# One-hot look-ups of a DLRM tower: whole-table one-hots, ids for two tables at once, two look-up banks, embedding copies on two engines

## The reference

```python
e = jnp.stack([tbl_0[ids[:, 0]], ..., tbl_25[ids[:, 25]]], axis=1)      # 2048 x 26 x 128
combined = jnp.concatenate([dense[:, None, :], e], axis=1)              # 2048 x 27 x 128
interactions = jnp.einsum('bnd,bmd->bnm', combined, combined)
z = jnp.concatenate([dense, interactions[:, _TRIU_I, _TRIU_J]], axis=1)
h = jnp.concatenate([z, dense], axis=1)
h = jnp.maximum(h @ W_top1 + b_top1, 0.0)
h = jnp.maximum(h @ W_top2 + b_top2, 0.0)
y = h @ W_top3
```

## Time and profile before

| | us |
|---|---|
| median of 3 runs | 602.59 (599.72 to 607.67) |
| the profiled execution | 605.72 |
| its span | 603.9 |
| mean granted clock of TensorE | 0.822 of full speed |

### The profile page before, as it was taken

The page is one execution under the profiler, slowest core; times in us unless marked ns, Lnnn a source line. Parts: engine busy times, 40 slices in busy tenths (PEclk is TensorE's granted clock), DMA queues, the critical chain, the costliest instruction groups (busy, mean ns, idle before and its releaser), DMA issues.

```text
span 603.9 us, 13994 instructions
## 1 busy us (share of the span) xinstructions
PE 433.2 (72%) x6369; PEld 389.7 (65%) x6369; DVE 263.3 (44%) x258; ACT 207.4 (34%) x313; POOL 253.8 (42%) x261
## 2 busy tenths in 40 slices
PE   3773277766788677787778778786777867787927
PEld 3672157655767667676667767675676766777827
DVE  5981035671544424535244434554154442465221
ACT  3550023443313333234222433233332333335713
POOL 7787545374423445154351644345433344500000
PEclk9886557987868788888787888896887878889978
DMA  8923113031102111031110311121111211101010
GB/s 202 243 55 104 39 32 99 21 108 37 27 25 83 45 33 41 18 92 33 27 45 16 101 34 27 37 86 47 29 26 29 85 42 33 41 7 58 4 58 1
DMA packets 21909, 32.79 MB, mean 54 GB/s; under 512 B 8030, under 2 KB 14846, under 8 KB 21850
## 3 DMA queue, kind: packets, MB, share of 16 engines
q0 software_dynamic: 8288, 16.83, 11.0%
q1 hardware_dynamic: 13562, 15.06, 8.8%
HBM read 28.24 MB, written 3.68 MB: 53 GB/s over the span
## 4 chain that ended last, share of the span: by engine, by line
PE 56%; issue 16%; DVE 12%; ACT 9%; another core or an unknown queue 6%; DMA 1%; SPq 0%; DVEq 0%
PE hot_ps L617 23%; PE gram_ps L642 11%; DVE one_hot L503 9%; PE mlp_ps L649 6%; PE transpose_ps L593 5%; PE mlp_ps L650 5%; PE mlp_ps L651 5%; ACT embed_t L424 4%; ACT embed_t L379 3%; PE hot_ids_ps L599 2%; DVE packed_lo L507 1%; DVE units L489 1%; DMA bounce<-units 1%; DMA rows<-bounce 1%
## 5 line engine op out<-in xcount | busy, mean ns | idle before, releaser
L351 POOL DMA_INDIRECT rows<-table,ids_sb x256 | 252.9, 988 | 272.9 <-PE transpose_ps L593 199.4
L617 PE MATMUL hot_ps<-one_hot,table_hi 125*128 125x256 f32 x640 | 200.2, 338 | 65.7 <-ACT embed_t L424 43.6
L503 DVE TENSOR_TENSOR one_hot<-hot_ids_ps,row_numbers_sb 125x1024 fp32r<-125x1024 f32 x160 | 192.4, 1236 | 110.9 <-PE hot_ids_ps L599 59.4
L617 PEld LDWEIGHTS hot_ps<-one_hot,table_hi 125*128 125x128 f32 x640 | 142.2, 222 | 81.3 <-DVE one_hot L503 46.0
L617 PE MATMUL hot_ps<-one_hot,table_lo 125*128 125x256 f32 x640 | 185.4, 315 | 0.0
L617 PEld LDWEIGHTS hot_ps<-one_hot,table_lo 125*128 125x128 f32 x640 | 143.5, 224 | 0.0
L642 PE MATMUL gram_ps<-embed_t 128*27 128x27 f32 x4096 | 77.3, 205 | 67.0 <-issue 66.1
L642 PEld LDWEIGHTS gram_ps<-embed_t 128*27 128x27 f32 x4096 | 58.8, 117 | 88.2 <-issue 85.3
L379 ACT COPY embed_t<-transpose_ps 128x512 f32<-128x512 f32 (+1 forms) x80 | 85.3, 1066 | 79.9 <-PE transpose_ps L593 51.1
L424 ACT COPY embed_t<-hot_ps 128x256 f32<-128x256 f32 x80 | 54.8, 684 | 148.2 <-PE hot_ps L617 82.1
L489 DVE COPY_PREDICATED units<-late_sb,gram_ps 128x208 f32<-128x208 int32 x32 | 35.1, 1098 | 121.2 <-ACT units L418 115.3
(11 more groups left out here) (49 smaller groups left out, 314.6 us busy)
## 6 DMA issues: line engine op xcount, KB each, us to landing
rows<-table,ids_sb POOLq DMA_INDIRECT x256
embed_t<-table SPq DMA_DIRECT2D x8, 448.0 KB
bounce<-units SPq DMA_DIRECT2D x8, 448.0 KB
scratch<-bounce SPq DMA_DIRECT2D x7, 378.0 KB
rows<-dense SPq DMA_DIRECT2D x16, 64.0 KB
scratch<-table SPq DMA_DIRECT2D x2, 448.0 KB
scratch<-w SPq DMA_DIRECT2D x1, 512.0 KB
scratch<-w_units SPq DMA_DIRECT2D x2, 252.0 KB
```

The source lines that it names most:

```text
L351: nc.gpsimd.indirect_dma_start(rows[:, t2, f, :], None, tables[table], bass.IndirectOffsetOnAxis(ids_sb[:, slot, table:table + 1], 0)).the ...
L503: nc.vector.tensor_tensor(one_hot[:, n % RING], ids_over, numbers_over, ALU.is_equal).then_inc(one_hot_ready, 1)
L617: last = nc.tensor.matmul(hot_ps[:, 0:GROUP], table[:, k % HOT, step, :], one_hot[:, (2 * k + half) % RING, j, :], start=(step == 0 and ta ...
```

## The change

- A one-hot is made for a whole table in one instruction of 2048 elements; the ring holds two whole tables. An H step is a whole table, and the order of the steps is written anew.
- The ids come in rows of 512, two tables side by side. One selector matmul spreads a pair; it stands ahead of the pair-before's second table.
- Even tables are looked up in `hot_ps`, odd ones in the half of `mlp_ps` that the odd MLP stages use. A table waits for the copy of the table two before, and odd tables and odd MLP stages wait for each other.
- Q0, Q2 and Q4 are copied out by ACT, Q1 and Q3 by DVE, with a semaphore each.
- To make room, `w1d_sb` goes (its piece is loaded into `scratch`, after `w2` is split), and one half of `hidden2` lies in `scratch`.

```diff
-RING = 3
-AHEAD = 2
+RING = 2
+PAIR = 2
+PAIRS = HOT // PAIR
+PAIR_ROWS = PAIRS * GROUPS
...
 STEPS = [
-    "D0 S0 M0 G0 Q0 G1 M1 G2 Q1 W0 M2 G3 H0 M3 H1 Q2 H2 W1 H3 Q3 H4 H5 W2 Q4 H6 H7".split(),
-    "G0 H8 G1 H9 Q0 H10 G2 H11 M4 G3 H12 Q1 H13 W3 M5 H14 Q2 H15 W4 M6 H16 Q3 H17 W5 Q4 H18 H19".split(),
+    "D0 S0 M0 G0 Q0 G1 M1 G2 Q1 W0 M2 W1 G3 H0 M3 Q2 W2 H1 Q3 H2 W3 Q4 H3".split(),
+    "G0 H4 W4 G1 Q0 H5 W5 M4 G2 Q1 M5 H6 G3 M6 Q2 H7 Q3 H8 Q4 H9".split(),
 ]
...
-FIRST_STEPS = "H0 H1 H2 Q0 H3 H4 H5 H6 Q1 H7 H8 H9 H10 Q2 H11 H12 H13 H14 Q3 H15 H16 H17 Q4 H18 H19".split()
+FIRST_STEPS = "H0 Q0 H1 H2 Q1 H3 H4 Q2 H5 H6 Q3 H7 H8 Q4 H9".split()
...
-    one_hot = sb("one_hot", [HOT_P, RING, HALF_STEPS, GROUP], F32R)
+    one_hot = sb("one_hot", [HOT_P, RING, HOT_STEPS, GROUP], F32R)
...
+        def hot_bank(k):
+
+            return hot_ps[:, 0:GROUP] if k % 2 == 0 else mlp_ps[:, 1, 0:GROUP]
...
                     sp.dma_start(scratch[:, :, :], w2.rearrange("(c p) h -> p c h", p=P)).then_inc(weights_loaded, 16)
+
+                    sp.wait_ge(weights_lo, CHUNKS + 1)
+                    sp.dma_start(w1d_sb, w1_dense).then_inc(weights_loaded, 16)
                     sp.dma_start(w1a_sb, w1_again).then_inc(weights_loaded, 16)
...
-                    sp.wait_ge(weights_lo, CHUNKS + 1)
-                    sp.wait_ge(w1_summed, 1)
+                    sp.wait_ge(weights_lo, len(pieces))
...
-            def make_one_hot(n):
...
+            def make_one_hot(k):
+
+                if k >= RING:
+
+                    dve.wait_ge(hot_ready, k - RING + 1)
+                if k % PAIR == 0:
+                    dve.wait_ge(hot_ids_ready, k // PAIR + 1)
+                ids = hot_ids_ps[0:HOT_P, None, k % PAIR * GROUP:(k % PAIR + 1) * GROUP]
+                nc.vector.tensor_tensor(one_hot[:, k % RING], ids.to_broadcast([HOT_P, HOT_STEPS, GROUP]),
+                                        row_numbers_sb[:, :, None].to_broadcast([HOT_P, HOT_STEPS, GROUP]),
+                                        ALU.is_equal).then_inc(one_hot_ready, 1)
+
+            def embed_copy(g, buf, t2, u):
+
+                dve.wait_ge(transposed, TRANSPOSE_USES * g + t2 * TILE_BANKS + u + 1)
+                nc.vector.tensor_copy(embed_target(g, t2, u), embed_source(t2, u)).then_inc(odd_copied, 1)
...
-                        elif step == "H" and LOOKUPS * (g + 1) + n + AHEAD < GROUPS * LOOKUPS:
-                            make_one_hot(LOOKUPS * (g + 1) + n + AHEAD)
+                        elif step == "Q" and n % 2 == 1:
+                            embed_copy(*next_tile(g, buf, t2), n)
+                        elif step == "H" and HOT * (g + 1) + n + RING < GROUPS * HOT:
+                            make_one_hot(HOT * (g + 1) + n + RING)
...
-            def broadcast_ids(k):
-
-                row = k % HOT * GROUPS + k // HOT
-                nc.tensor.matmul(hot_ids_ps[0:HOT_P, 0:GROUP],
-                                 selector[:, row:row + 1].to_broadcast([HOT * GROUPS, HOT_P]), hot_ids_sb[:, :],
+            def broadcast_ids(pair):
+
+                row = pair % PAIRS * GROUPS + pair // PAIRS
+                nc.tensor.matmul(hot_ids_ps[0:HOT_P, :],
+                                 selector[:, row:row + 1].to_broadcast([PAIR_ROWS, HOT_P]), hot_ids_sb[:, :],
                                  start=True, stop=True).then_inc(hot_ids_ready, 1)
...
+                k = g * HOT + n
+
+                pe.wait_ge(one_hot_ready, k + 1)
...
+                if k % PAIR == PAIR - 1 and k + 1 < GROUPS * HOT:
+
+                    broadcast_ids(k // PAIR + 1)
+                if k >= 2:
+
+                    pe.wait_ge(hot_copied, k - 1)
+                if k % 2 == 1 and odd_bank["stages"]:
+
+                    pe.wait_ge(mlp_copied, odd_bank["stages"])
+                for step in range(HOT_STEPS):
                     for table in (table_hi, table_lo):
...
                 pe.wait_ge(mlp_copied, MLP_USES * g + need + 1)
+                if m % 2 == 1:
+
+                    pe.wait_ge(hot_copied, odd_bank["tables"])
+                    odd_bank["stages"] = MLP_USES * g + m + 2
```

More of the change, by code:

```diff
@@ L199, in dlrm_tower @@
         transposed = sem("transposed")
-        embed_copied = sem("embed_copied")
+        even_copied = sem("even_copied")
+        odd_copied = sem("odd_copied")
         gram_ready = sem("gram_ready")
@@ L420, in hot_copy @@
             def hot_copy(g, k, buf):
-                act.wait_ge(hot_ready, LOOKUPS * g + 2 * (k + 1))
+                act.wait_ge(hot_ready, HOT * g + k + 1)
                 out = over_group(g, HOT_FEATURE + k)
-                nc.scalar.copy(out, hot_ps[:, 0:GROUP].rearrange("p (t b) -> p t b", t=TILES)).then_inc(hot_copied, 1)
+                nc.scalar.copy(out, hot_bank(HOT * g + k).rearrange("p (t b) -> p t b", t=TILES)).then_inc(hot_copied, 1)
             def group(g, buf, steps, mlp_before=True):
@@ L430, in group @@
                             late_columns(g, buf, t2 * TILE_ROUNDS + n // PARTS)
-                        elif step == "Q":
+                        elif step == "Q" and n % 2 == 0:
                             embed_copy(*next_tile(g, buf, t2), n)
-                        elif step == "H" and n % 2 == 1:
-                            hot_copy(g + 1, n // 2, 1 - buf)
+                        elif step == "H":
+                            hot_copy(g + 1, n, 1 - buf)
                         elif step == "D" and mlp_before:
@@ L462, in _ @@
             for step, n in [(x[0], int(x[1:])) for x in FIRST_STEPS]:
-                if step == "H" and n % 2 == 0 and n // 2 + 1 < HOT:
-                    split_hi(n // 2 + 1)
-                elif step == "H" and n % 2 == 1:
-                    hot_copy(0, n // 2, 0)
-                elif step == "Q":
+                if step == "H":
+                    if n + 1 < HOT:
+                        split_hi(n + 1)
+                    hot_copy(0, n, 0)
+                elif n % 2 == 0:
                     embed_copy(0, 0, 0, n)
@@ L563, in _ @@
             for step, n in [(x[0], int(x[1:])) for x in FIRST_STEPS]:
-                if step == "H" and n % 2 == 0 and n // 2 + 1 < HOT:
-                    split_lo(n // 2 + 1)
                 if step == "H":
-                    make_one_hot(n + AHEAD)
+                    if n + 1 < HOT:
+                        split_lo(n + 1)
+                    make_one_hot(n + RING)
+                elif n % 2 == 1:
+                    embed_copy(0, 0, 0, n)
             dve.wait_ge(late_loaded, 16)
@@ L581, in _ @@
         def _(pe):
+            odd_bank = {"tables": 0, "stages": 0}
             def transposes(g, buf, t2, u, first=False):
@@ L588, in transposes @@
                 pe.wait_ge(gathered[t2][u], 16 * len(gathers(u)) * (g + 1))
-                if not (first and use < 2):
-                    pe.wait_ge(embed_copied, TRANSPOSE_USES * g + use - 1)
+                if u >= 2 or not first:
+                    done, at = (TILES * g + t2, u - 2) if u >= 2 else (TILES * g + t2 - 1, u - 2 + TILE_BANKS)
+                    if at % 2 == 0:
+                        pe.wait_ge(even_copied, even_copies(done, at + 1))
+                    else:
+                        pe.wait_ge(odd_copied, odd_copies(done, at + 1))
                 for i, f in enumerate(features(u)):
@@ L621, in look_up @@
                 last.then_inc(hot_ready, 1)
-                if half == 0 and k + 1 < GROUPS * HOT:
-                    pe.wait_ge(one_hot_ready, 2 * (k + 1))
-                    broadcast_ids(k + 1)
+                if k % 2 == 1:
+                    odd_bank["tables"] = k + 1
             def gram(g, buf, t2, n, first):
@@ L682, in mlp @@
                         for c in range(H2_CHUNKS):
-                            last = nc.tensor.matmul(out[:, t:t + 1], hidden2[:, c, t * P:(t + 1) * P], w3_sb[:, c:c + 1],
+                            last = nc.tensor.matmul(out[:, t:t + 1], hidden2[c][:, t * P:(t + 1) * P], w3_sb[:, c:c + 1],
                                                     start=(c == 0), stop=(c == H2_CHUNKS - 1))
@@ L763 @@
     given = {
-        "dense": a["r_dense_features"], "ids": a["ids"], "hot_ids": np.ascontiguousarray(a["ids"].T[HOT_TABLES]).reshape(HOT * GROUPS, GROUP),
+        "dense": a["r_dense_features"], "ids": a["ids"], "hot_ids": np.ascontiguousarray(a["ids"].T[HOT_TABLES].reshape(PAIRS, PAIR, GROUPS, GROUP).transpose(0, 2, 1, 3)).reshape(
+            PAIR_ROWS, PAIR * GROUP),
         "row_numbers": np.arange(HOT_ROWS, dtype=np.float32).reshape(HOT_P, HOT_STEPS),
```

68 lines of the change are left out of this document (28 added, 40 removed).

## The result

The changed kernel takes **609.13 us** (median of 20 runs, 604.14 to 620.14) where the kernel before takes 601.93 (20 runs). The ratio is 1.0113, 95% interval 1.0083 to 1.0142: a loss of 1.1% that the measurement can tell from none. I had forecast a small gain, 600 against 602.6.

A forecast was written before the change was run, and what follows sets the result against it. PE bounds the kernel, over a quarter of its time waiting, with each group's second tile hanging on gathers. Six steady groups by -0.5 is -3, plus 1, minus 2: 4 us less, 601.7, scaled 598.6, rounded up to 600; range 568 to 624.

The forecast's parts named there:

- Ends: Step on the run's start and last group: plus 1 us for weights, 0 for first tables and grams, minus 2 at the end.
- 1 us of a range of 0 to 3.15: Start: the first weights piece loads later, once `w2` is split, delaying DVE's later one-hots; 1 us taken.
- two copies (2.4 us) come on top: First ten tables, DVE-paced: two added copies, 2.4 us, counted 0 because the first grams stand among the first 48 gathers anyway.
- 2 us less for the edge without one-hots: Last group: no one-hots are left to make at the edge, so 2 us less.
- 10 us of cover: Group edge: SyncE's pack, twice some 3.15 us from the predicated copy on, has 10 us of cover.
- The edge wait of 4 to 8 us: Each group's edge: PE waits 4 to 8 us for DVE, where 2.2 stood before.
- The two late one-hots at the edge: Group's end: two one-hots see PE's signals late out of the gather run, by 1.7 to 6 us; 3.7 taken.
- The DVE copy at 1.2 us: Embedding copies moved to DVE: a 128x512 copy out of PSUM takes near 1.2 us, ACT's time for the same access.
- The steady group at no gain to speak of: Steady groups, tile 1 at 35.0 against 35.4 us and tile 0 at 0: a gain of 0.4 to 0.5 us each.
- The hold is PE's own waiting (faster): Rival, gather runs: signals are late because PE stands at a semaphore, two banks end it; 572 us, chance 0.35.
- The queue of DVE at the edge (slower): Rival, group edge: `dense_lo` stands behind four one-hots, two late; 620 us, chance 0.25; sign: DVE's "remote" waits before the last two.
- Two banks give nothing: Rival, look-ups: 2.3 us of short waits are only renamed to one-hot waits; 603 us, chance 0.40 together with the forecast's case.

The follow-up runs named there:

- c1: The changed kernel itself, unaltered, in the free condition (kernel before 430.48 us there): 443.42 us, ratio 1.0323.
- c2: The kernel before, unaltered, traced in the same free condition: 432.36 us (one run).
- e7: Changed kernel with the last weight pieces' steps (w2 and two more) moved later, behind grams; held condition: 614.93 us, ratio 1.0170 to the kernel before.
- e10: Kernel before with two look-up banks alone, no other part of the change; held condition: 626.28 us, ratio 1.0345.
- e5: Changed kernel with tile 1's last gram ahead of M5 and H6 on every engine; free condition: 436.34 us, ratio 1.0170 to the kernel before.
- e8: e6 and e7 together, with the first tables' two odd embedding copies on ACT; held condition: 589.95 us, ratio 0.9731 to the kernel before.
- e6: Changed kernel with e5 and e1 together and DVE's packed split ahead of both last one-hots; free condition: 408.69 us, ratio 0.9508 to the kernel before.
- e3: Changed kernel with a single look-up bank, each table waiting for ACT's copy of the one before; free condition: 447.63 us, ratio 1.0458.
- e13: e10's kernel with GpSimd's gathers left out, SyncE loading consecutive rows instead; free condition: 429.78 us, ratio 0.9991 to the kernel before.
- e11: Kernel before with GpSimd's 256 gathers left out, SyncE loading consecutive rows instead; free condition: 435.03 us, ratio 1.0105.
- e1: Changed kernel with the dense split moved behind M6 and the packed split ahead of the last look-up; free condition: 439.87 us, ratio 1.0258.

## Why the prediction was wrong

The sum by its own terms, between the same marks, in us:

| stretch | forecast | held | free (c1 less c2) |
|---|---|---|---|
| start, to group 2 | +0.5 (1, less 0.5 for group 1) | +5.8 | +6.3 |
| groups 2 to 5 | -2 | +0.1 | +4.4 |
| group 6, with the edge behind it | -2.5 (0.5, and 2 for the edge) | -1.6 | -1.1 |
| from group 7 on | 0 | +3.2 | +1.6 |
| sum | -4 | +7.5 | +11.2 |

**The step that failed is "Ends".** It put +1 at the start, and nothing at all behind the last edge. What the runs show in its place are two waits that the new order makes.

*The start.* For the weights I took 1 us of a range of 0 to 3.15, thinking of a later load. What came is another mechanism: the step that splits `w2` now stands ahead of Q4's copy, ACT waits nearly 5 us for the landing, and PE's gram begins at 106.43, right behind that copy, after 3.9 us of idle (3.6 when free). e7, which moves that step, begins group 1 4.6 us and group 2 3.0 us earlier. The first group's own edge, 7.4 us of wait where the kernel before has 2.65, had no term either. For the look-ups I wrote "two copies (2.4 us) come on top" and counted 0. When free, the first gram is 3.4 us later, since besides the two copies DVE waits for the pairs' broadcasts. When held, the 0 is neither shown nor refuted. In the changed kernel's profile the look-ups run into the gathers and the gram behind them waits less, but e7 has the same order without that, and e10 has it with the order of before. So nothing shows that the change makes it.

*The end.* I wrote 2 us less for the edge without one-hots, and group 6 is indeed 1.6 us shorter. But the pack, of which I had said that it has 10 us of cover, is late there: PE waits 2.2 us for `packed_lo` in place of 0.4, since the one-hots that covered the pack elsewhere are missing while its predicated copy is still queued behind the one of H6. The stretch behind it takes 4.2 us more, at a clock of 0.77 in place of 0.99 [windows above], of which the rest of the run gives 1.0 back. When free the same stretch is 27.98 us at 0.77 against 25.09 at 0.86, and e5, with the copy ahead of H6 and the wait down to 0.4, takes 25.42. So the wait accounts for some 2.6 us, and the rest of the 4.2 goes with the clock, which differs between the two profiles of the kernel before as well; why stays open.

**What held.** The edge wait of 4 to 8 us: 7.0 to 7.4, at each of six edges. The two late one-hots at the edge, taken at 3.7 us: 3.2 (2.63 and 0.60 above). The DVE copy at 1.2 us: 1.18 (32 of them). The Trainium skill's rule ("VectorE: DVE Perf Modes", the TRN2 errata) gives the estimate of 0.66 us; the trace differs by 0.5 us, and the measurement decides. ACT's bank waits gone, gram's "issue" over 50 us: 67.9. The steady group at no gain to speak of: four groups within 0.1 us. That was luck in part. Tile 1, which I had at 35.0 us for 35.4, takes 36.7 between the marks of the earlier trace rows in one group (248.36 to 285.10), and tile 0, which I had unchanged, gives that back. Without the hold the change costs 1.1 us per group net, and the 1 us that I had for half clock behind the edge is 2.0 there.

**The rivals.** "The hold is PE's own waiting (faster)" fell: e10 has the second bank alone and is 3.4% slower, and e8 took the edge's waits away, and in both gram's waits under "issue" grew (27.4 to 44.4 and 37.4 to 51.0 us in four groups). "The queue of DVE at the edge (slower)" had mechanism and place right, and its sign, "remote" waits ahead of the last two one-hots, was there. e6 shows the worth: 5 us per group when free, once the pack was freed too. Its price of 620 was too high held, where clearing the edge gave 1.5 us per group (e8). "Two banks give nothing" is nearly so: e3 makes them worth 4.2 us of 443 free, e10 a loss of 3.4% alone and held. The Trainium skill reports of one matmul kernel that PSUM double-buffering gave no further gain ("TensorE: Matmul & The Clock Gate", HAM oscillation); e13 against e11 comes near that, e3 does not.

## What to carry over

A wait that is removed is worth what the next chain to the same point leaves: here two chains, DVE's queue and the pack, ended at nearly the same time, and in the free condition freeing one gave 0.8 or 1.6% (e1, e5) and both, with one split moved further, 7.8% (e6). List every producer of the first instruction behind the seam and free them together; short splits that the other engine waits for go ahead of long preparatory work in an in-order queue. Walk the prologue and the last group as closely as the steady loop: ask of each step that waits for a load what is queued behind it, and of each chain called covered whether the covering work is still there in the last group. And before a late signal in one trace is put down to an edit, look whether another run with the same order has it.

## What was unexpected of the hardware

The same kernel before took 608 us on one chip and 430.56 on the same chip later; the difference goes with gathers in flight. Windows of the kernel before: one group with 32 gathers, one with 16, one stretch with none, held:

```profile
421.61:494.22 72.61, 54.51 (x797) 49.26 (x797) 30.98 (x31) 24.15 (x37) 30.43 (x32) 0.84 0.16 43
494.22:556.76 62.54, 50.53 (x796) 46.27 (x796) 28.41 (x29) 24.17 (x37) 15.32 (x16) 0.86 0.12 34
```

and the same places free (c2):

```profile
285.42:333.37 47.95, 41.77 (x794) 38.75 (x794) 29.90 (x30) 24.06 (x37) 30.25 (x32) 1.00 0.24 66
333.37:381.52 48.15, 42.95 (x795) 39.70 (x796) 28.28 (x29) 24.07 (x37) 17.34 (x18) 0.96 0.17 47
381.52:406.61 25.09, 19.99 (x609) 18.23 (x610) 7.31 (x10) 12.27 (x21) 0.00 (x0) 0.86 0.01 3
```

24.7 us more with 32 gathers, 14.4 more with 16 (18 begun, free), none more with none (23.54 us above): some 0.8 to 0.9 us of hold per gather, while a gather itself takes the same time in both (988 ns). In the stretch of the earlier trace rows the free kernel takes 25.64 us with its gathers and 25.35 without. What the hold strikes in the start is not fixed by the order of the steps: in e7 it strikes the first grams, in the changed kernel the look-ups ahead of them. Whether it is the indirect transfer, GpSimd's queue or something outside this core that makes the hold stays open, since no run without gathers met it.
